# Third product for bank B made one place earlier, and the sum from bank B taken ahead of the first quarter's maximum

## What is computed

```python
Q = (img_embed @ Wq).reshape(B, -1, H, D).transpose(0, 2, 1, 3)
K = (sent_embed @ Wk).reshape(B, -1, H, D).transpose(0, 2, 1, 3)
V = (sent_embed @ Wv).reshape(B, -1, H, D).transpose(0, 2, 1, 3)
score = jnp.einsum('bhqd,bhkd->bhqk', Q, K) / math.sqrt(D)
score = jnp.where(mask, score, -jnp.inf)
attn = jax.nn.softmax(score, axis=-1)
ctx = jnp.einsum('bhqk,bhkd->bqhd', attn, V).reshape(B, -1, H * D)
out = ctx @ Wo + img_embed
# then mean and variance over the last axis, (out - mu) * rsqrt(var + EPS) * gamma + beta
```

## Time and profile before

| what | us |
|---|---|
| time, median of 3 runs | 356.77 (356.71 to 357.55) |
| the profiled execution | 356.75 |
| its span, first to last instruction | 355.0 |
| TensorE busy (matmul) | 348.2, 98% |
| weight loads busy | 323.6, 91% |
| VectorE busy | 269.3, 76% |
| ScalarE busy | 231.2, 65% |
| GpSimd busy | 192.9, 54% |
| mean granted TensorE clock | 0.996 of 2.4 GHz |

### The profile page before, as it was taken

How to read it: one execution, slowest core, us unless ns; L and a number is a source line. 1 busy time by engine, 2 the same in 40 slices (tenths; PEclk the granted TensorE clock), 3 DMA queues, 4 the chain that set the end, 5 groups by cost and what they waited for, 6 DMA issues and landing times. The chain is left out here.

```text
span 355.0 us, 6790 instructions
## 1 busy us (share of the span) xinstructions
PE 348.2 (98%) x2271; PEld 323.6 (91%) x2271; DVE 269.3 (76%) x501; ACT 231.2 (65%) x780; POOL 192.9 (54%) x208
## 2 busy tenths in 40 slices
PE   8999999999999999999999999999999999999994
PEld 6999999999999999988899889889988998899883
DVE  3299998673911267898798888987987989789895
ACT  3377764244333669877786876877778868768560
POOL 0045640000003858679769688688696796885243
PEclk9999999999999999999999999999999999999998
DMA  7998679766644080043141341440532413413012
GB/s 262 409 423 318 254 238 348 266 245 210 225 152 187 0 292 6 3 178 116 64 176 54 126 151 50 160 144 35 179 100 80 162 65 130 149 41 110 31 49 100
DMA packets 19682, 55.80 MB, mean 157 GB/s; under 512 B 1728, under 2 KB 3264, under 8 KB 17728
## 3 DMA queue, kind: packets, MB, share of 16 engines
q1 hardware_dynamic: 18784, 54.38, 42.7%
q10 hardware_dynamic: 864, 1.00, 0.9%
HBM read 46.98 MB, written 8.39 MB: 156 GB/s over the span
## 5 line engine op out<-in xcount | busy, mean ns | idle before, releaser
L628 PE MATMUL pair<-vw_hi,pt_hi 128*128 128x512 f32 x155 | 62.2, 401 | 0.0
L628 PE MATMUL pair<-vw_hi,pt_lo 128*128 128x512 f32 x155 | 61.0, 393 | 0.0
L628 PE MATMUL pair<-vw_lo,pt_hi 128*128 128x512 f32 x155 | 60.7, 392 | 0.0
L1230 POOL TENSOR_TENSOR out_sb<-centred,beta_sb 128x512 f32<-128x512 f32 x30 | 38.8, 1293 | 26.8 <-ACT centred L820 26.7
L1250 POOL TENSOR_TENSOR x_sum<-xt_in 128x256 f32<-128x256 f32 x16 | 11.9, 745 | 62.2 <-DMA xt_in<-x_tiles 62.0
L775 ACT ACTIVATE prob<-c,neg_max 128x77 f32<-128x77 f32 x128 | 43.9, 346 | 0.0
L1275 POOL TENSOR_TENSOR xo_lo<-x_sum,xo_hi 128x512 fp32r<-128x512 f32 x32 | 41.2, 1293 | 0.5 <-ACT xo_hi L799 0.5
L557 PE MATMUL pair<-a_hi,xo_hi 128*128 128x308 f32 x128 | 40.4, 316 | 0.0
L813 ACT ACTIVATE pt_hi<-pair 128x640 fp32r<-128x640 f32 x32 | 22.5, 702 | 26.9 <-PE pair L615 26.9
L557 PE MATMUL pair<-a_lo,xo_hi 128*128 128x308 f32 x128 | 38.9, 304 | 0.0
L1076 DVE TENSOR_TENSOR pair<-pair,x_in 128x512 f32<-128x512 f32 x31 | 21.7, 700 | 22.6 <-PE pair L628 22.4
(11 more groups left out here) (117 smaller groups left out, 958.7 us busy)
## 6 DMA issues: line engine op xcount, KB each, us to landing
w_out<-wo SPq DMA_DIRECT2D x8, 1024.0 KB, 4.8
xt_in<-x_tiles SPq DMA_DIRECT2D x16, 512.0 KB, 4.1
x_in<-x_rows SPq DMA_DIRECT2D x16, 512.0 KB, 4.8
out<-out_sb SPq DMA_DIRECT2D x31, 256.0 KB, 2.2
w_out<-wq_t SPq DMA_DIRECT2D x7, 1024.0 KB, 6.9
w_proj<-wv SPq DMA_DIRECT2D x8, 768.0 KB, 4.6
w_proj<-wk SPq DMA_DIRECT2D x6, 768.0 KB, 9.2
w_out<-wq_t SPq DMA_DIRECT2D x2, 512.0 KB, 7.6
```

What stands on the lines that cost most here:

```text
L628: mm = pe.matmul(ps_out[:, i % 2, 0:s.model], ps[:, j, :], v[:, b, j, :], start=(j == 0 and n == 0), stop=(j == s.key_t - 1 and n == len(p ...
L1230: pool.tensor_tensor(out_sb[i % OUT_RING][:, :], centred[i % 2][:, :], beta_sb[:, :], ALU.add)\
```

## The change

`second_products` is split into `product_s3` (the third product for bank B) and `last_products` (S4 and A22), each with the waits that it had. In pairs 2 to 15 TensorE now makes S3 ahead of A12, so the order of the four is S3, A12, S4, A22. In pairs 0 and 1 the order stays. The waits of `combine_c22` and `max_c11` are counted anew for it: S3 is the fifth product in pairs 0 and 1 and the fourth after that, A12 the other way round. VectorE does `combine_c22` ahead of `max_c11` in pairs 2 to 15.

```diff
+        def s3_done(p):
+
+            return nth_product(p, 5 if p < 2 else 4)
+
+        def c11_done(p):
+
+            return nth_product(p, 4 if p < 2 else 5)
...
-            def second_products(p):
+            def product_s3(p):
 
                 b = batch_of(p)
                 pe.wait_ge(act_xo_hi, SPLITS * p + 4)
                 pe.wait_ge(pool_xo_lo, SPLITS * p + 3)
                 pe.wait_ge(dve_comb, COMBINED * p + 1)
                 product(p, bank_b, S3, t_at(t_hi, a_hi, T3, b), t_at(t_lo, a_lo, T3, b))
+
+            def last_products(p):
+
+                b = batch_of(p)
                 pe.wait_ge(dve_comb, COMBINED * p + 2)
                 product(p, bank_d, S4, right(a_hi, b, 1, 1), right(a_lo, b, 1, 1))
...
                 transpose_prob(a - 1)
+                product_s3(p)
                 product_on_a(p)
-                second_products(p)
+                last_products(p)
                 out_rows(a - 2)
...
             def combine_c22(p):
-                dve.wait_ge(pe_prod, PRODUCTS * p + 5)
+                dve.wait_ge(pe_prod, s3_done(p))
...
             def max_c11(p):
                 a = 2 * p
-                dve.wait_ge(pe_prod, PRODUCTS * p + 4)
+                dve.wait_ge(pe_prod, c11_done(p))
...
+                combine_c22(p)
                 max_c11(p)
-                combine_c22(p)
                 centre(a - 3, ps_out[:, (a - 3) % 2, 0:s.model])
```

More of the change, by code:

```diff
@@ L313, in value_of, with nth_product @@
             return kv_full if u < FULL_OUT else v_t[u % 2][:, :, :]
+        def nth_product(p, n):
+            return PRODUCTS * p + n
+        def s3_done(p):
+            return nth_product(p, 5 if p < 2 else 4)
+        def c11_done(p):
+            return nth_product(p, 4 if p < 2 else 5)
         def use_w_out(u):
@@ L671, in _ @@
             product_on_a(0)
-            second_products(0)
+            product_s3(0)
+            last_products(0)
             first_products(1)
@@ L675, in _ @@
             transpose_prob(0)
-            second_products(1)
+            product_s3(1)
+            last_products(1)
             pe.wait_ge(dve_vw_lo, len(groups))
```

## The result

The changed kernel takes 356.06 us (median of 6 runs, 355.40 to 356.19), the kernel before 357.15 us in the runs beside it (median of 6, 356.71 to 357.56). The ratio is 0.9967, with a 95% interval of 0.9957 to 0.9977: 1.1 us faster. The interval lies clear of no change, but it spans the prediction's bound of 0.3%, so the gain is about as large as the smallest that was to be called one. In a later set of executions of both kernels the ratio was 0.9967 again (0.9955 to 0.9980).

A forecast was written before the change was run, and what follows sets the result against it. TensorE's stream was taken as the bound. Wins at A22 of 0.38 (pair 2), 0.22 (pair 6) and 0.66 (eleven pairs), 1.26 less 0.02, took 1.24 off 356.77: 355.53, say 355.5 us; range 355.0 to 356.5.

The forecast's parts named there:

- the prediction's bound of 0.3%: Smallest difference from no change that a measurement of this kernel tells, 1.07 us; faster meant below 355.70 us.
- The two steps across A22's start: TensorE, from S4's last matmul to A22's second: 0.34 us in steady pairs before, predicted 0.28 in pairs 3 to 14.
- the stretch: From pair 2's fourth product (first matmul) to pair 15's A22 (last matmul), by starts; the pairs' stretch was predicted 1.2 to 1.3 us shorter.
- the 356.3 of two rivals: Total if A22's second condition keeps its price (chance 0.13), or S3's new wait costs 0.06 per pair (0.09).
- Pair 2: The tight pair at A22: its loss of 0.38 us counted as won whole, with a residue of 0 to 0.06.
- The rule of the Trainium skill: VectorE's next operation waits until the pipe is empty; c22 would start some 0.08 us later in pair 2.
- Pair 15: Its 0.06 us at A22 wins nothing: the next transposition, already waiting for VectorE's division, waits 0.06 longer.
- the rival of a new wait: S3's three conditions behind the transposition cost 0.06 (356.3 us) or 0.22 (358.4 us) in each of 13 pairs; chance 0.15.
- that cover: Idle time of ScalarE and VectorE absorbing the first four exponentials' 0.47 us delay; cost nothing, 0 to 0.05 in the tail.
- The rival of the second condition: A22's 0.06 us is the price of waiting for two engines; only 0.48 us goes, 356.3 us; chance 0.13.
- a fixed distance from c22's end: A22's load starts 0.11 to 0.12 us after c22's end in pairs with different losses, so it is a wait.
- What S2 shows: Evidence against the second condition's price: product S2 has conditions from three engines, yet its two steps show no loss.

The follow-up runs named there:

- the small dose: Changed kernel with an unused VectorE maximum over 4 x 50 elements ahead of c22 in pairs 2 to 15; 356.36 us, one execution.

## Why the prediction was right

**The bound and the place.** TensorE's stream was the bound, and its losses stood where the spacing of starts put them. The two steps across A22's start shrank by 1.37 us over pairs 2 to 15; 0.01 is left in pair 2 and nothing in the others. The forecast's 1.26 us for pairs 2 to 14 and 0.06 for pair 15 are 1.32; the stretch gained 1.36, a little more than the 1.2 to 1.3 that the prediction had named as a sign. c22 came 0.44 us earlier after its residual in pair 5 (1.79 us for 2.23), inside the 0.40 to 0.48 named. Forecast and stretch agree better than they should: the other steps of the four products grew by 0.13 us in all, and the output rows, of which one block in each of three pairs had run 0.06 us slow in the first trace, gave 0.10. Against the second trace of the kernel before the gain is 1.26.

**The time.** The sum gave 355.53 us, and 356.06 was measured: inside the range, but 0.53 us above the sum and above the 355.70 that the prediction had set as the edge of faster. Of that, 0.38 is the kernel before, which took 357.15 us in the runs beside it and not 356.77; the other 0.15 is a gain of 1.09 us in place of 1.24. So the gain is the fair comparison, and the time by itself would prove little: 356.06 is nearer to the 356.3 of two rivals than to the forecast. What tells them apart are the two steps at A22 and the start of S3 in the trace.

**Pair 2.** Predicted a residue of 0 to 0.06, measured 0.01 and 0.02 in the two traces. The rule of the Trainium skill (VectorE: DVE Perf Modes, The DRAIN you can't avoid) would have kept 0.06. c22 started at 151.27, while the addition ahead of it ran to 151.32, so the trace again shows a start before that end. Counted from the residual it started 0.03 us later than the maximum had (1.79 us for 1.76 in pair 5), and in pair 2, which had no lead, this made the residue.

**Pair 15.** Predicted that its 0.06 comes back as a longer wait of the next transposition. It did: 0.31 us for the 0.25 of the earlier trace rows.

```profile
337.15 0.31 PEld L631 LDWEIGHTS pair<-identity,prob 128*128 128x128 f32 x3 [0.31 <-DVE prob L1079]
```

**What was moved earlier.** S3 starts 0.47 us behind the transposition, as A12 did in the earlier trace rows, and its three conditions cost nothing, so the rival of a new wait is out:

```profile
190.64 0.71 PE L631 MATMUL pair<-identity,prob 128*128 128x128 f32 x5
191.11 0.39 PE L569 MATMUL pair<-a_hi,xo_hi 128*128 128x308 f32 x1
```

**What was moved later.** In pair 5 the four exponentials came 0.49 us later against the residual (2.76 us after it for 2.28), the second four 0.20 later, and ScalarE's 1.05 us of idle time in the earlier trace rows is 0.84. The later maximum fitted into c22's old slot, and the centring kept its place. The experiment with the maximum later still shows that in the tail that cover would have ended within the next 0.59 us.

**The rival of the second condition** had 0.13 and deserved more thought. The evidence that I gave against it (a fixed distance from c22's end) held for both stories. What S2 shows is that conditions long met cost nothing; it could not show what two conditions cost when the one on the semaphore instruction is the last to be met.

**The one thing under-weighed** is how near the sum lies to the bound of what can be told: 1.24 us forecast and 1.09 measured stand against 1.07. That the ratio came out beyond the bound and not just inside it is partly luck.

## What to carry to other kernels

Where matmuls follow one another, look for a waiting step in the spacing of starts, not in busy time or in the list of waits, and check it by the distance from the end of the work waited for to the next load: one distance in pairs with different losses is a wait. When a product must wait for another engine to read the bank it adds onto, put one more product between, and move that reader to the front of its own engine's queue; alone, TensorE's half made this kernel 1.5% slower and VectorE's half gained nothing (1.0148 and 1.0009). If a step waits for two engines and one of them is long done, put that condition on an earlier step: it took 0.06 us off each wait that counted (0.9986).

## What was not expected of the hardware

- A load that waits for two engines started 0.115 to 0.117 us after the last of them was done (all 16 pairs with TensorE's order alone), one that waits for that engine alone 0.052 to 0.053 us (pairs 2 to 15 of the kernel before with one condition). The difference is a semaphore instruction of 0.05 us ahead of the load, and it counts only when the condition on it is the last to be met.
- A stall of VectorE of 0.25 us between two small steps, which nothing in the profile explains, is in pair 6 in the traces of before and after. With one instruction more per pair on VectorE it is in pair 13 (the small dose's 304.09, where it costs 0.05 us). It is there once in pairs 2 to 15 of each of the thirteen traces, always ahead of the addition to the variance, so it goes with the program and not with the execution. Counted with VectorE's semaphore instructions, it stands at the 320th of 687 instructions in the nine traces without an added one, and at the 576th of 701 in the four with one: 256 places later. In each of these kernels the other of the two places shows no stall; there VectorE stands behind an instruction of 0.47 us or has just waited 1.1 us or more for TensorE. Something that recurs every 256 instructions and shows only between short ones would fit. What it is was not tried.
- In the changed kernel's first trace the step from A12 to S4 takes 0.152 us in pairs 2 to 7 and 0.143 in pairs 8 to 15, which read the matrix of the other batch; the old order had its long step (0.149) elsewhere, inside S4. The pairs of the first batch lost 0.02 us each by the new order's steps. Why was not tried.
